# Two input-scale banks instead of four in the first FFN round, and the second convolution stage's output sums split between VectorE and GpSimd

## The chip, the cores and the metric

The kernel runs on one core of a Trainium2 chip. The metric is the device time of one execution in microseconds (us); for the kernel before it is the median of three runs. TensorE (PE) multiplies matrices into PSUM, VectorE (DVE) and ScalarE (ACT) work elementwise on PSUM and SBUF, GpSimd (POOL) elementwise on SBUF, and SyncE (SP) issues the DMAs. Engines wait for each other on counting semaphores that the kernel sets.

## The reference

A block of three residual parts over x of 2048 tokens by 1024 features, all in float32:

```
x = x + 0.5 * ffn(layernorm(x))
x = x + attention(layernorm(x))      # opens with a convolution over 3 tokens, 1024 -> 768
x = x + 0.5 * ffn(layernorm(x))      # the same weights as the first

def ffn(x):
    routing = softmax(x @ gate_w.T)                       # 8 experts
    in_scale, out_scale = routing @ in_channel_scale, routing @ out_channel_scale
    return x * in_scale @ sign(weight).T * out_scale + bias

def attention(x):
    q, k, v = split(conv3(x, conv_w) + conv_b, 3)         # 256 wide each
    # 16 heads of 64, causal softmax inside blocks of 128 tokens, then two projections
```

## The kernel before

Four phases run one after the other: FFN, convolution, attention, FFN. Tensors carry a prefix in the profile: `f_` for both FFNs, `c_` for the convolution, `a_` for attention. A float32 operand is split into a high part (rounded to the matmul's input format) and a low part (the rest), so that two or three fast matmuls give a product at nearly full precision.

**FFN.** Tokens go in 8 groups of 256. For each group TensorE transposes the normalised tokens (L587), ScalarE copies them to `f_xT` (L487), TensorE makes the router's logits (L597, L604), and the softmax's result comes back as `f_rT` (L499). Then, for each of 8 chunks k of 128 features, a chain of four steps makes the matmul's input: `in_scale` (L621, TensorE) writes the chunk's scales into 256 columns of a PSUM bank; `scale` (L343, VectorE) multiplies them by the tokens into the bank's other half; `high` (L504, ScalarE) rounds that half to `f_a_hi`; `low` (L348, VectorE) subtracts and leaves `f_a_lo`. VectorE's program has the order scale(k), low(k-1). The products follow (L638).

In every round but the first, `scale_bank` gives two banks, those of `f_p_s`, in turn, and in_scale(k) waits for low(k-2). This work for the next group lies between products of the group before. The first round has no products to lie between: it runs once at the start of each FFN, before the first product. There `scale_bank` gives four banks (the two of `f_p_s`, then `f_p_n` and `f_p_t`), and in_scale(k) waits for low(k-4) alone. Behind the chain ScalarE copies the next group's logits (L491), TensorE turns them (L604), makes an output scale (L626) and starts the products.

**Convolution.** The sequence is cut into groups of four outputs, which are computed from a few transformed products (stages j = 0, 1, 2), with 6 output chunks c in each stage: 18 units n. A unit makes two results in PSUM, `first` and `second`, in one of two pairs of banks, from 4 ring entries of filters (3 slots). An entry takes TensorE 12 matmuls. Filters of the second stage are the sum and difference of what GpSimd added (`outer_sum`, L785) and the middle tap: `sums(n)` (L989, L990, VectorE), then ScalarE rounds (`high`, L880) and VectorE subtracts (`finish`, L1000) into the ring. The filter half n arrives by DMA; its load waits until `sums(n-2)` is done in stage 2, and for `finish` in stage 3. In VectorE's program of stage 2 an odd n has finish(n,0), add((n-3)//2), finish(n,1).

`add(n)` takes a unit's results. In stage 2 ScalarE first writes two scaled copies of `second` to SBUF (`c_room`, L909, L910). VectorE then has six instructions: two that combine `first` with these copies and write back into the PSUM banks (L1024, L1025), and four that add the results to the four output planes `c_Y` (L1028 to L1032). TensorE may overwrite the banks after the sixth. GpSimd has only its `outer_sum` in this stage.

Between stage 2 and 3 VectorE and ScalarE also have 16 chunks of input data to split (L1012, L892), and SyncE loads four attention weights of 1 MB each (L837) behind the load of filter half 27, before that of half 28.

## Time and profile before

| | |
|---|---|
| median of 3 runs | 1117.16 us (1112.67 to 1117.47) |
| the profiled execution's own time, its span | 1117.16 us, 1115.4 us |
| mean granted TensorE clock | 0.931 of full speed |
| busy share of the span | PE 85%, DVE 64%, ACT 41%, POOL 33% |
| HBM read and written | 89.21 MB and 31.46 MB |

The span runs from the first to the last instruction; what lies around it is 1.76 us. The phases lie about at 0 to 250 us (FFN), 250 to 495 us (convolution), 495 to 910 us (attention) and from 910 us on (FFN). A matmul row's length is its own duration from first to last column; back-to-back matmuls overlap, so a row of 0.39 us can follow the one before by 0.23 us.

### The profile page before, as it was taken

How to read it: one execution, taken by the hardware profiler on the slowest of the kernel's cores; microseconds unless marked ns; L12 is line 12 of the kernel's file. 1: busy time of each engine (PE TensorE's matmuls, PEld its weight loads, DVE VectorE, ACT ScalarE, POOL GpSimd, SP SyncE). 2: the span in 40 equal slices, each digit the busy share in tenths (PEclk: the TensorE clock that was granted, in tenths of full speed). 3: DMA queues.
4: the chain of work that ended last, by engine and by line, in shares of the span. 5: the costliest groups of instructions: out<-in, count | busy, mean ns of one | idle time of the engine just before them, and what ended most of it. 6: DMA issues, size and time to landing. Idle time of an engine off the chain costs nothing. (4 is left out here: it accounts for less than half of the span.)

```text
span 1115.4 us, 15622 instructions
## 1 busy us (share of the span) xinstructions
PE 952.7 (85%) x4960; PEld 716.4 (64%) x4960; DVE 718.2 (64%) x1469; ACT 452.8 (41%) x1127; POOL 371.6 (33%) x305
## 2 busy tenths in 40 slices
PE   4898888868898998967978996998799746999997
PEld 3576666653335876845766785886678634678786
DVE  6677775477998885532774587288458447576652
ACT  3534444431244352323763454356345305433431
POOL 2245555564542200000223131133214411355555
PEclk9799999988999999986988997998899885999999
DMA  8333322322323426533002112121101258154243
GB/s 280 127 133 114 113 75 76 132 95 85 113 94 135 168 66 245 207 133 113 2 19 76 39 57 76 38 75 65 48 38 58 95 165 279 58 189 149 78 132 113
DMA packets 44781, 121.45 MB, mean 109 GB/s; under 512 B 5936, under 2 KB 18224, under 8 KB 43312
## 3 DMA queue, kind: packets, MB, share of 16 engines
q1 hardware_dynamic: 44720, 120.68, 31.4%
q8 instruction: 33, 0.54, 0.2%
q14 instruction: 28, 0.23, 0.1%
HBM read 89.21 MB, written 31.46 MB: 108 GB/s over the span
## 5 line engine op out<-in xcount | busy, mean ns | idle before, releaser
L638 PE MATMUL f_p_m<-f_wsign,f_a_hi 128*128 128x512 f32 x512 | 209.0, 408 | 0.0
L638 PE MATMUL f_p_m<-f_wsign,f_a_lo 128*128 128x512 f32 x512 | 203.1, 397 | 0.0
L1342 POOL TENSOR_TENSOR a_s<-a_s,a_sums 128x512 f32<-128x512 f32 x64 | 66.6, 1041 | 252.7 <-DVE a_sums L1481 252.7
L270 POOL TENSOR_TENSOR f_y<-f_y,f_res 128x512 f32<-128x512 f32 x64 | 82.7, 1293 | 147.3 <-DVE f_y L469 147.1
L1549 PE MATMUL a_p_g<-a_xs_hi,x_room 128*128 128x512 f32 x256 | 102.4, 448 | 22.8 <-DVE a_xs_lo L1433 22.2
L1397 ACT ACTIVATE a_s<-a_s,a_nmx 128x128 f32<-128x128 f32 x256 | 99.3, 390 | 39.1 <-DVE a_nmx L1477 39.0
L638 PEld LDWEIGHTS f_p_m<-f_wsign,f_a_hi 128*128 128x128 f32 x512 | 97.6, 191 | 22.6 <-issue 4.1
L638 PEld LDWEIGHTS f_p_m<-f_wsign,f_a_lo 128*128 128x128 f32 x512 | 97.7, 191 | 16.8
L1114 PE MATMUL c_p_m<-c_vf,c_ring_f 128*128 128x512 f32 x192 | 86.8, 609 | 9.5 <-DVE c_ring_f L792 6.4
L343 DVE TENSOR_TENSOR f_p_s<-f_xT,f_p_s 128x256 f32<-128x256 f32 x120 | 50.2, 424 | 65.9 <-PE f_p_s L621 65.2
L504 ACT CAST f_a_hi<-f_p_s 128x256 fp32r<-128x256 f32 x120 | 44.5, 376 | 107.1 <-DVE f_p_s L343 106.3
L1116 PE MATMUL c_p_m<-c_vh,c_ring 128*128 128x512 f32 x192 | 76.8, 400 | 8.7 <-DVE c_ring L1000 6.9
L267 POOL TENSOR_TENSOR f_res<-f_res,f_hbias 128x512 f32<-128x512 f32 x64 | 83.3, 1302 | 0.0
L1549 PEld LDWEIGHTS a_p_g<-a_xs_hi,x_room 128*128 128x128 f32 x256 | 53.0, 207 | 39.3 <-DVE a_xs_lo L1433 21.3
L469 DVE TENSOR_TENSOR f_y<-f_p_m,f_oscale 128x512 f32<-128x512 f32 x64 | 43.9, 686 | 51.3 <-PE f_p_m L638 51.3
L1117 PE MATMUL c_p_m<-c_vl,c_ring 128*128 128x512 f32 x192 | 76.0, 396 | 0.0
L1118 PE MATMUL c_p_m<-c_vh,c_ring 128*128 128x512 f32 x192 | 75.9, 396 | 0.0
L1114 PEld LDWEIGHTS c_p_m<-c_vf,c_ring_f 128*128 128x128 f32 x192 | 36.8, 195 | 59.1 <-issue 52.2
L487 ACT COPY f_xT<-f_p_t 128x512 f32<-128x512 f32 x56 | 33.1, 592 | 82.6 <-PE f_p_t L587 82.6
L587 PE MATMUL f_p_t<-ident,f_xin 128*128 128x128 f32 x224 | 38.6, 300 | 31.0 <-DVE f_xin L310 26.2
L785 POOL TENSOR_TENSOR c_raw<-c_raw 128x512 f32<-128x512 f32 x24 | 35.7, 1491 | 73.0 <-DMA c_raw<-in_conv_w_dram 48.8
L1472 DVE TENSOR_TENSOR a_s<-a_p_s,a_mask 128x512 f32<-128x512 f32 x64 | 43.7, 683 | 20.9 <-PE a_p_s L1573 20.8
(178 smaller groups left out, 2066.5 us busy)
## 6 DMA issues: line engine op xcount, KB each, us to landing
c_raw<-in_conv_w_dram SPq DMA_DIRECT2D x24, 768.0 KB, 4.3
f_y<-in_w_t_dram SPq DMA_DIRECT2D x16, 512.0 KB, 7.9
f_res<-in_x_dram SPq DMA_DIRECT2D x16, 512.0 KB, 3.8
x_after_ffn<-f_y SPq DMA_DIRECT2D x8, 1024.0 KB, 6.0
f_res<-x_after_attention SPq DMA_DIRECT2D x16, 512.0 KB, 3.9
out_dram<-f_y SPq DMA_DIRECT2D x8, 1024.0 KB, 6.1
f_xin<-in_x_dram SPq DMA_DIRECT2D x7, 1024.0 KB, 7.6
a_residual<-x_after_ffn SPq DMA_DIRECT2D x14, 512.0 KB, 3.5
```

What stands on the lines that cost most here:

```text
L267: pool.tensor_tensor(res[:, t, h], res[:, t, h], hbias[:, h], ALU.add).then_inc(res_biased, 1)
L270: pool.tensor_tensor(y[:, p, t, h], y[:, p, t, h], res[:, t, h], ALU.add).then_inc(y_done, 1)
L343: dve.tensor_tensor(bank[:, FTOK:HALF], xT[:, p, k, :], bank[:, 0:FTOK], ALU.mult).then_inc(scaled, 1)
L504: act.copy(a_hi[:, p, k, :], scale_bank(g, k)[:, FTOK:HALF]).then_inc(hi_done, 1)
L638: last = pe.matmul(p_m[:, q % 2, :], part[:, p, k, q // 2 * P:q // 2 * P + P], wsign[:, k, q % 2 * HALF:q % 2 * HALF + HALF], start=(k == ...
L1114: last = pe.matmul(out, ring_f[:, slot, 0, cols], vf[:, f, k, :], start=start, stop=stop)
L1116: pe.matmul(out, ring[:, slot, 0, cols], vh[:, f, k, :], start=start, stop=False)
L1117: pe.matmul(out, ring[:, slot, 0, cols], vl[:, f, k, :], start=False, stop=False)
L1118: last = pe.matmul(out, ring[:, slot, 1, cols], vh[:, f, k, :], start=False, stop=stop)
L1342: pool.tensor_tensor(s[:, r], s[:, r], sums[:, r].unsqueeze(2).broadcast_to([P, 4, P]), ALU.mult).then_inc(probs_ready, 1)
L1397: done = act.activation(s[:, r, h, :], s[:, r, h, :], ACT.Exp, bias=nmx[:, r, h:h + 1], scale=SCALE, accum_out=sums[:, r, h:h + 1])
L1549: mm = pe.matmul(p_g[:, bank, :], a, b, start=n == 0, stop=n == len(pairs) - 1)
```

## The change

Three parts. (1) `scale_bank` is gone: the first round uses the two banks of `f_p_s` as all others do, and in_scale(k) waits for low(k-2) there too. The waits that kept `f_p_n` and `f_p_t` apart from their other users go with it. (2) In stage 2 of the convolution the combined results go to `c_room` in SBUF instead of PSUM; VectorE adds two of the four planes and GpSimd the other two, between its `outer_sum`s. (3) TensorE may overwrite `first` after the two combining instructions, and `second` after ScalarE's copies. SyncE's stores wait for the split counters.

```diff
-        def scale_bank(g, k):
-            if first_round(g):
-                return (p_s[:, 0, :], p_s[:, 1, :], p_n[:], p_t[:])[k % 4]
-            return p_s[:, k % 2, :]
...
                 def in_scale(g, p, k):
                     pe.wait_ge(r_copied, g + 1)
-                    if not first_round(g):
-                        wait(pe, lo_done, 8 * g + k - 1)
-                    elif k >= 2:
-                        wait(pe, lo_done, k - 3)
-                        pe.wait_ge(t_copied, 8)
-                    pe.matmul(scale_bank(g, k)[:, 0:FTOK], ics3[:, k * P:k * P + P], rT[:, p, :],
+                    wait(pe, lo_done, 8 * g + k - 1)
+                    pe.matmul(p_s[:, k % 2, 0:FTOK], ics3[:, k * P:k * P + P], rT[:, p, :],
...
+                def add(c):                                   # GpSimd
+                    n = NCH + c
+                    pool.wait_ge(first_taken, n + 1)
+                    pool.wait_ge(y_scaled, c + 1)
+                    pool.tensor_tensor(Y[:, c, 2], room[:, 0], Y[:, c, 2], ALU.add)
+                    pool.tensor_tensor(Y[:, c, 3], room[:, 1], Y[:, c, 3], ALU.add).then_inc(out_added, 1)
...
                 for n in range(2 * NCH, 4 * NCH):
                     conv.outer_sum(pool, n)
+                    if n % 2 == 0 and n >= 2 * NCH + 4:
+                        add((n - 2 * NCH - 4) // 2)
+                add(NCH - 2)
+                add(NCH - 1)
...
                     if j == 1:                                # ScalarE, before it writes room
-                        wait(act, y_added, 5 * c - 3)
+                        wait(act, y_added, 2 * c)
+                        wait(act, out_added, c)
...
                     if j == 1:                                # VectorE
                         dve.wait_ge(second_taken, n + 1)
-                        dve.scalar_tensor_tensor(second, first, -1.0 / 6, room[:, 1], ALU.mult, ALU.subtract).then_inc(y_added, 1)
-                        dve.scalar_tensor_tensor(first, first, -1.0 / 6, room[:, 0], ALU.mult, ALU.add).then_inc(y_added, 1)
+                        dve.scalar_tensor_tensor(room[:, 0], first, -1.0 / 6, room[:, 0], ALU.mult, ALU.add)
+                        dve.scalar_tensor_tensor(room[:, 1], first, -1.0 / 6, room[:, 1], ALU.mult, ALU.subtract).then_inc(first_taken, 1)
+                        dve.wait_ge(first_taken, n + 1)
                         dve.wait_ge(y_scaled, c + 1)
-                        dve.wait_ge(y_added, 5 * c + 1)
-                        dve.tensor_tensor(Y[:, c, 1], second, Y[:, c, 1], ALU.add).then_inc(y_added, 1)
-                        dve.tensor_tensor(Y[:, c, 3], second, Y[:, c, 3], ALU.add).then_inc(y_added, 1)
-                        dve.wait_ge(y_added, 5 * c + 2)
-                        dve.tensor_tensor(Y[:, c, 0], first, Y[:, c, 0], ALU.add).then_inc(y_added, 1)
-                        dve.tensor_tensor(Y[:, c, 2], first, Y[:, c, 2], ALU.add).then_inc(first_taken, 1)
+                        dve.tensor_tensor(Y[:, c, 0], room[:, 0], Y[:, c, 0], ALU.add).then_inc(y_added, 1)
+                        dve.tensor_tensor(Y[:, c, 1], room[:, 1], Y[:, c, 1], ALU.add).then_inc(y_added, 1)
...
                     if f == 0:                                # TensorE, before it overwrites a bank
                         pe.wait_ge(first_taken, n - 1)
-                    elif n - 2 < NCH:
+                    elif n - 2 < 2 * NCH:
                         pe.wait_ge(second_taken, n - 1)
-                    elif n - 2 < 2 * NCH:
-                        pe.wait_ge(first_taken, n - 1)
```

TensorE's program in the first round of an FFN, before the change (lines of the kernel before; the first two rows are in_scale for k = 0 and 1, the last the first product):

```order
L621 MATMUL f_p_s<-f_rT,f_ics 128x256 [waits f1_r_copied]
L597 MATMUL f_p_r<-f_xT,f_gateT 32x256 [waits f1_r_copied,f1_t_copied]
L597 MATMUL f_p_r<-f_xT,f_gateT 32x256 x7
L621 MATMUL f_p_n<-f_rT,f_ics 128x256 [waits f1_t_copied,f1_r_copied]
L621 MATMUL f_p_t<-f_rT,f_ics 128x256 [waits f1_t_copied,f1_r_copied]
L621 MATMUL f_p_s<-f_rT,f_ics 128x256 [waits f1_t_copied,f1_lo_done,f1_r_copied] x2
L621 MATMUL f_p_n<-f_rT,f_ics 128x256 [waits f1_t_copied,f1_lo_done,f1_r_copied]
L621 MATMUL f_p_t<-f_rT,f_ics 128x256 [waits f1_t_copied,f1_lo_done,f1_r_copied]
L604 MATMUL f_p_r<-f_four_to_one,f_logT 128x8 [waits f1_l_copied]
```

And now, in the changed kernel's own line numbers (L608 is in_scale, L588 the logits, L595 their turn):

```order
L608 MATMUL f_p_s<-f_rT,f_ics 128x256 [waits f1_r_copied]
L588 MATMUL f_p_r<-f_xT,f_gateT 32x256 [waits f1_r_copied,f1_t_copied]
L588 MATMUL f_p_r<-f_xT,f_gateT 32x256 x7
L608 MATMUL f_p_s<-f_rT,f_ics 128x256 [waits f1_lo_done,f1_r_copied] x6
L595 MATMUL f_p_r<-f_four_to_one,f_logT 128x8 [waits f1_l_copied]
```

The order is the same; six in_scales wait for a `low` where four did, and each for one two chunks back.

GpSimd's program in stage 2, now (L772 is `outer_sum`, L853 and L854 the new additions; before, `outer_sum` stood alone in all these rows); the first row is outer_sum(16):

```order
L772 TENSOR_TENSOR c_raw<-c_raw 128x512 [waits c_raw_loaded0]
L853 TENSOR_TENSOR c_Y<-c_room,c_Y 128x512 [waits c_y_scaled,c_first_taken]
L854 TENSOR_TENSOR c_Y<-c_room,c_Y 128x512
L772 TENSOR_TENSOR c_raw<-c_raw 128x512 [waits c_raw_loaded1]
L772 TENSOR_TENSOR c_raw<-c_raw 128x512 [waits c_raw_loaded0]
L853 TENSOR_TENSOR c_Y<-c_room,c_Y 128x512 [waits c_y_scaled,c_first_taken]
L854 TENSOR_TENSOR c_Y<-c_room,c_Y 128x512
```

outer_sum(17) and outer_sum(18) now stand behind an addition that waits for VectorE.

VectorE's program there, now, from a unit's combining instructions to the next unit's (L1025, L1026 combine; L1029, L1030 add planes; L1001 is `finish`, L990 and L991 are `sums`):

```order
L1025 SCALAR_TENSOR_TENSOR c_room<-c_p_m,c_room 128x512 [waits c_second_taken]
L1026 SCALAR_TENSOR_TENSOR c_room<-c_p_m,c_room 128x512
L1029 TENSOR_TENSOR c_Y<-c_room,c_Y 128x512 [waits c_y_scaled,c_first_taken]
L1030 TENSOR_TENSOR c_Y<-c_room,c_Y 128x512
L1001 TENSOR_TENSOR c_ring<-c_p_u,c_ring 128x512 [waits c_filter_high]
L990 TENSOR_TENSOR c_p_u<-c_raw 128x512 [waits c_filter_ready,c_outer_made]
L991 TENSOR_TENSOR c_p_u<-c_raw 128x512
L1001 TENSOR_TENSOR c_ring<-c_p_u,c_ring 128x512 [waits c_filter_high] x2
L990 TENSOR_TENSOR c_p_u<-c_raw 128x512 [waits c_filter_ready,c_outer_made]
L991 TENSOR_TENSOR c_p_u<-c_raw 128x512
L1001 TENSOR_TENSOR c_ring<-c_p_u,c_ring 128x512 [waits c_filter_high]
```

Two plane additions are left where four stood, and both now read two SBUF tensors, where each read one from PSUM (`c_p_m`).

## Rows read from the trace of the kernel before

**Rows 1.** The page, part 1: busy time, share of the span and instructions of each engine.

```profile
PE 952.7 (85%) x4960; PEld 716.4 (64%) x4960; DVE 718.2 (64%) x1469; ACT 452.8 (41%) x1127; POOL 371.6 (33%) x305
```

**Rows 2.** Timeline, first FFN: start us, us, engine, line, operation [idle before <-releaser].

```profile
29.02 0.58 PE L621 MATMUL f_p_n<-f_rT,f_ics 128*128 128x256 f32 x1
29.08 0.42 DVE L348 TENSOR_TENSOR f_a_lo<-f_p_s,f_a_hi 128x256 fp32r<-128x256 f32 x1
29.64 0.43 DVE L343 TENSOR_TENSOR f_p_n<-f_xT,f_p_n 128x256 f32<-128x256 f32 x1
...
32.96 0.42 DVE L343 TENSOR_TENSOR f_p_t<-f_xT,f_p_t 128x256 f32<-128x256 f32 x1
...
34.12 1.02 PE L604 MATMUL f_p_r<-f_four_to_one,f_logT 128*128 128x8 f32 x4 [1.74 <-ACT f_logT L491]
...
38.98 0.90 PE L587 MATMUL f_p_t<-ident,f_xin 128*128 128x128 f32 x4
```

**Rows 3.** Timeline, a later round of the same FFN, where two banks are used.

```profile
73.72 0.41 DVE L348 TENSOR_TENSOR f_a_lo<-f_p_s,f_a_hi 128x256 fp32r<-128x256 f32 x1
...
74.61 0.43 DVE L343 TENSOR_TENSOR f_p_s<-f_xT,f_p_s 128x256 f32<-128x256 f32 x1 [0.48 <-PE f_p_s L621]
```

**Rows 4.** Timeline, first round of the second FFN.

```profile
939.67 0.42 DVE L348 TENSOR_TENSOR f_a_lo<-f_p_s,f_a_hi 128x256 fp32r<-128x256 f32 x1
...
943.80 0.42 DVE L343 TENSOR_TENSOR f_p_t<-f_xT,f_p_t 128x256 f32<-128x256 f32 x1
```

**Rows 5.** Windows: stretch, busy PE, PEld, DVE, ACT, POOL, granted clock, DMA share, GB/s.

```profile
32.00:34.00 2.00, 0.37 (x1) 0.08 (x1) 1.88 (x7) 1.33 (x5) 0.00 (x0) 0.50 0.99 393
942.00:944.00 2.00, 0.71 (x2) 0.34 (x2) 2.00 (x7) 1.12 (x3) 0.00 (x0) 1.00 0.99 379
944.00:946.00 2.00, 1.05 (x5) 1.05 (x6) 1.89 (x5) 1.75 (x4) 0.00 (x0) 0.53 0.48 195
```

**Rows 6.** Timeline, first convolution stage and its end: DVE and POOL.

```profile
276.08 1.26 POOL L785 TENSOR_TENSOR c_raw<-c_raw 128x512 f32<-128x512 f32 x1 [0.55 <-ACT c_raw L777]
276.13 1.76 DVE L792 SCALAR_TENSOR_TENSOR c_ring_f<-c_raw 128x512 f32<-128x512 f32 x1
...
341.24 1.54 POOL L785 TENSOR_TENSOR c_raw<-c_raw 128x512 f32<-128x512 f32 x1 [2.72 <-DMA c_raw<-in_conv_w_dram]
341.56 1.75 DVE L1007 TENSOR_TENSOR c_vl<-X,c_vh 128x512 fp32r<-128x512 f32 x1
```

**Rows 7.** Timeline, second convolution stage: DVE, POOL and ACT.

```profile
365.10 0.70 DVE L1024 SCALAR_TENSOR_TENSOR c_p_m<-c_p_m,c_room 128x512 f32<-128x512 f32 x1 [0.48 <-ACT c_room L910]
...
368.54 1.29 POOL L785 TENSOR_TENSOR c_raw<-c_raw 128x512 f32<-128x512 f32 x1 [1.75 <-DMA c_raw<-in_conv_w_dram]
368.70 0.68 DVE L1000 TENSOR_TENSOR c_ring<-c_p_u,c_ring 128x512 fp32r<-128x512 f32 x1
374.19 0.59 ACT L880 CAST c_ring<-c_p_u 128x512 fp32r<-128x512 f32 x1 [2.13 <-DVE c_p_u L990]
375.98 0.70 DVE L1024 SCALAR_TENSOR_TENSOR c_p_m<-c_p_m,c_room 128x512 f32<-128x512 f32 x1 [0.48 <-ACT c_room L910]
```

**Rows 8.** Timeline, from the second convolution stage into the third.

```profile
418.41 0.47 PE L1116 MATMUL c_p_m<-c_vh,c_ring 128*128 128x512 f32 x1 [0.79 <-issue]
...
424.25 0.69 DVE L1024 SCALAR_TENSOR_TENSOR c_p_m<-c_p_m,c_room 128x512 f32<-128x512 f32 x1
427.85 1.28 DVE L1000 TENSOR_TENSOR c_ring<-c_raw,c_ring 128x512 fp32r<-128x512 f32 x2
428.58 0.50 PE L1116 MATMUL c_p_m<-c_vh,c_ring 128*128 128x512 f32 x1 [1.17 <-DVE c_ring L1000]
430.97 0.43 SPq L772 DMA_DIRECT2D c_raw<-in_conv_w_dram  x1
444.31 1.14 ACT L880 CAST c_ring<-c_raw 128x512 fp32r<-128x512 f32 x2 [9.27 <-DMA c_raw<-in_conv_w_dram]
445.80 0.76 PE L1116 MATMUL c_p_m<-c_vh,c_ring 128*128 128x512 f32 x1 [3.31 <-DVE c_ring L1000]
```

More of the change, by code:

```diff
@@ L339, in scale @@
                 def scale(g, p, k):
-                    bank = scale_bank(g, k)
                     dve.wait_ge(s_full, 8 * g + k + 1)
-                    dve.tensor_tensor(bank[:, FTOK:HALF], xT[:, p, k, :], bank[:, 0:FTOK], ALU.mult).then_inc(scaled, 1)
+                    dve.tensor_tensor(p_s[:, k % 2, FTOK:HALF], xT[:, p, k, :], p_s[:, k % 2, 0:FTOK], ALU.mult).then_inc(scaled, 1)
                 def low(g, p, k):
@@ L347, in low @@
                     wait(dve, m_full, 4 * g - 4)
-                    dve.tensor_tensor(a_lo[:, p, k, :], scale_bank(g, k)[:, FTOK:HALF], a_hi[:, p, k, :].bitcast(F32),
+                    dve.tensor_tensor(a_lo[:, p, k, :], p_s[:, k % 2, FTOK:HALF], a_hi[:, p, k, :].bitcast(F32),
                                       ALU.subtract).then_inc(lo_done, 1)
@@ L503, in high @@
                     wait(act, m_full, 4 * g - 4)
-                    act.copy(a_hi[:, p, k, :], scale_bank(g, k)[:, FTOK:HALF]).then_inc(hi_done, 1)
+                    act.copy(a_hi[:, p, k, :], p_s[:, k % 2, FTOK:HALF]).then_inc(hi_done, 1)
                 def sign_w(k):
@@ L580, in transposes @@
                     wait(pe, t_copied, 4 * g + q - two)
-                    if isinstance(g, int) and g == 2 and q == 0:
-                        pe.wait_ge(lo_done, 8)
                     bank = p_n if two and q % 2 else p_t
@@ L804, in conv_phase @@
     first_taken, second_taken = sem("first_taken"), sem("second_taken")
-    y_scaled, y_added, y_final = sem("y_scaled"), sem("y_added"), sem("y_final")
+    y_scaled, y_added, out_added, y_final = sem("y_scaled"), sem("y_added"), sem("out_added"), sem("y_final")
     y_stored = sem("y_stored")
@@ L841, in _ @@
                         sp.wait_ge(first_taken, 2 * NCH + c + 1)
-                        sp.wait_ge(y_added, 5 * c + 5)
+                        sp.wait_ge(y_added, 2 * c + 2)
+                        sp.wait_ge(out_added, c + 1)
                         sp.dma_start(Yd[c], Y[:, c].rearrange("p s m -> p (s m)")).then_inc(y_stored, 16)
@@ L846, in _ @@
                     sp.wait_ge(first_taken, 2 * NCH + c + 1)
-                    sp.wait_ge(y_added, 5 * c + 5)
+                    sp.wait_ge(y_added, 2 * c + 2)
+                    sp.wait_ge(out_added, c + 1)
                     sp.dma_start(Yd[c], Y[:, c].rearrange("p s m -> p (s m)")).then_inc(y_stored, 16)
@@ L1023, in add @@
                         dve.wait_ge(second_taken, n + 1)
-                        dve.scalar_tensor_tensor(second, first, -1.0 / 6, room[:, 1], ALU.mult, ALU.subtract).then_inc(y_added, 1)
-                        dve.scalar_tensor_tensor(first, first, -1.0 / 6, room[:, 0], ALU.mult, ALU.add).then_inc(y_added, 1)
+                        dve.scalar_tensor_tensor(room[:, 0], first, -1.0 / 6, room[:, 0], ALU.mult, ALU.add)
+                        dve.scalar_tensor_tensor(room[:, 1], first, -1.0 / 6, room[:, 1], ALU.mult, ALU.subtract).then_inc(first_taken, 1)
+                        dve.wait_ge(first_taken, n + 1)
                         dve.wait_ge(y_scaled, c + 1)
-                        dve.wait_ge(y_added, 5 * c + 1)
-                        dve.tensor_tensor(Y[:, c, 1], second, Y[:, c, 1], ALU.add).then_inc(y_added, 1)
-                        dve.tensor_tensor(Y[:, c, 3], second, Y[:, c, 3], ALU.add).then_inc(y_added, 1)
-                        dve.wait_ge(y_added, 5 * c + 2)
-                        dve.tensor_tensor(Y[:, c, 0], first, Y[:, c, 0], ALU.add).then_inc(y_added, 1)
-                        dve.tensor_tensor(Y[:, c, 2], first, Y[:, c, 2], ALU.add).then_inc(first_taken, 1)
+                        dve.tensor_tensor(Y[:, c, 0], room[:, 0], Y[:, c, 0], ALU.add).then_inc(y_added, 1)
+                        dve.tensor_tensor(Y[:, c, 1], room[:, 1], Y[:, c, 1], ALU.add).then_inc(y_added, 1)
                     if j == 2:
                         dve.wait_ge(chunk_used, 16 * n + 16)
-                        dve.wait_ge(y_added, 5 * c + 5)
+                        dve.wait_ge(y_added, 2 * c + 1)
+                        dve.wait_ge(out_added, c + 1)
                         dve.scalar_tensor_tensor(Y[:, c, 0], first, 0.25, Y[:, c, 0], ALU.mult, ALU.add).then_inc(first_taken, 1)
```

## The prediction, made before the changed kernel ran

> **What bounds the kernel now.** The page's first part comes first: TensorE is busy for 85% of the span [rows 1], and where it isn't, each gap has one cause. So an edit counts where it lengthens or shortens a gap of TensorE. The change touches two places in each of which TensorE hardly works: the first round of each FFN, where the timeline shows no product yet, and the second convolution stage with its end. I read the timeline of both, engine by engine.
>
> In the first round of the first FFN the reader is to see that VectorE sets the pace. TensorE issued in_scale(2) at 29.02, before low(0) ended at 29.08 + 0.42 = 29.50, into a third bank; scale(2) began at 29.64, scale(7) at 32.96 [rows 2]. That is 5 steps in 3.32 us, 0.66 each, and one `scale` and one `low` are queued at 0.33 each. The granted clock was 0.50, 1.2 GHz [rows 5]. Behind scale(7) come high(7), ScalarE's copy of the logits, then TensorE's L604, which sat idle 1.74 us for that copy [rows 2], and all first products. Nothing of the kernel runs ahead of this chain, so what it loses the program loses.
>
> In stage 2 of the convolution TensorE runs without a gap: two units' combining instructions began at 365.10 and 375.98, 10.88 us apart [rows 7], which is 48 matmuls at 0.227. VectorE has slack there. At the end of the stage it has none: TensorE sat idle 0.79 at 418.41 and 1.17 at 428.58 for a ring entry that VectorE finished late, and 3.31 at 445.80 for filter half 28, which was issued at 430.97 behind the attention weights and reached ScalarE only at 444.31 [rows 8].
>
> **Part 1, two banks in the first round.** Now in_scale(k) waits for low(k-2), and VectorE's program has low(k-2) right before scale(k). So VectorE waits for the whole way over TensorE and back. This is seen in a later round, where two banks are in use: low ended at 73.72 + 0.41 = 74.13 and the next scale began at 74.61, 0.48 later, at 2.4 GHz [rows 3]. At 1.2 GHz the matmul is longer: from 29.02 to the scale at 29.64 it is 0.62 [rows 2], and with 0.05 to 0.1 for the semaphore 0.69. A step is then 0.33 (scale) + 0.42 (low) + 0.69 = 1.44 us at 1.2 GHz and 1.23 at 2.4 GHz, against 0.66.
> - First FFN: scale(2) at 29.50 + 0.69 = 30.19, scale(7) five steps later at 37.39, against 32.96 [rows 2]: +4.4 us. The clock was low in this stretch [rows 5] and TensorE gets even less to do.
> - Second FFN: low(0) ended at 940.09 [rows 4]. scale(2) at 940.8; steps 3 to 5 at 1.23, since the clock was 1.00 in 942 to 944, and 6 and 7 at 1.44, since it was 0.53 in 944 to 946 [rows 5]: scale(7) at 947.3 against 943.80 [rows 4], +3.5 us.
> Together +7.9 us. Bounds: five steps that cost only 0.57 more and a free start are 2.9 per FFN, five at 0.78 and a full start 4.4; so +5.8 to +8.8. The dropped waits on `f_p_n` and `f_p_t` were long fulfilled and give nothing. Nothing covers this: ScalarE's signs of the weights, the normalising and the second softmax stand behind the chain on their own engines and move with it.
>
> **Part 2, the plane additions.** On paper VectorE loses two instructions of 0.6 in each unit, less about 0.1 for waiting for its own combining instruction: 1.1 us. In stage 2 this meets slack. At its end it would count twice, for add(10) and add(11), since VectorE works there without a pause: half 28 would be issued 2.1 us sooner and TensorE's start at 445.80 come 2.1 us sooner. That is the gain side, -2.1.
>
> But the additions left on VectorE now read two SBUF tensors, and GpSimd starts its own in the same moment, on the same semaphore. What such a meeting costs is in the trace. GpSimd began at 276.08 and ended at 277.34; a VectorE instruction with two SBUF operands that began at 276.13 took 1.76 instead of 0.68 and ended at 277.89, 0.55 after GpSimd. Where VectorE was first, GpSimd's instruction took 1.54 instead of 1.29, and VectorE's next, 1.75 [rows 6]. Beside a VectorE instruction with one operand in PSUM nothing is lost: 0.68 at 368.70 within GpSimd's 368.54 to 369.83 [rows 7]. So in a meeting of two-SBUF instructions one waits for the other. (The Trainium skill says the same in "SBUF — State Buffer", section "SBUF: two separate sides": the port pair that VectorE and GpSimd share is an exclusive lock for the whole instruction, which a VectorE op with two SBUF inputs needs too; by that rule the offload is no gain, without it the sum is -2.1. The trace agrees with the rule at 276.13, 1.76 us.)
>
> Counted from T, the start of a unit's first combining instruction, with 1.15 us for a GpSimd instruction after VectorE lets go and 0.55 for VectorE after GpSimd:
> - combining 0 to 1.30; VectorE's first addition to 2.05; GpSimd's first to 3.15; VectorE's second to 3.7; GpSimd's second to 4.8;
> - finish (one operand in PSUM) runs meanwhile, but sums(17) needs outer_sum(17), which now stands behind GpSimd's additions: to 6.05. outer_sum(18) follows without a pause, to 7.35, as its filter has landed; it meets sums(17), whose first half then ends at 7.9, the second at 8.5;
> - two finishes to 9.7, sums(18) to 10.9, one finish to 11.5: the next T.
> VectorE and GpSimd together need 11.55 us for what TensorE does in 10.88. The first needed entry would be ready at 365.10 + 9.15 = 374.25, and TensorE wanted it at about 374.19, when it let go of the entry before [rows 7]. From there the lateness grows by 0.67 per unit over two more units (after the fourth, no second outer_sum stands in the way): 0.1, 0.8, 1.5. TensorE ends stage 2 1.5 us late.
>
> At the end of the stage: after add(10) the first data split, an instruction with two SBUF operands, meets GpSimd's second addition, and ends at T + 5.3 to 5.5 instead of T + 4.8: +0.6. After add(11) the same meets the finish that TensorE waited for at 428.58; its source is now SBUF, so it ends at T + 5.3, where it ended 427.85 + 0.68 - 424.25 = 4.28 after T [rows 8]: +1.0. Half 28 and all behind it come later by 1.5 + 0.6 + 1.0 = 3.1 us, and from 445.80 on TensorE has only its own work. Bounds for the convolution: -2.1 (no meeting costs) to +6, if a cycle takes one more 1.07 of blocking (three cycles, 3.2, less what doesn't reach TensorE). I take +3.1, nearest to rows 6.
>
> **Part 3, banks released sooner** is worth nothing: six instructions from 365.10 are over by 368.8, and TensorE returns to those banks at about 374.19, when the unit between is done [rows 7]; at the stage's end it waits for ring entries, not for banks.
>
> **Sum.** +7.9 + 3.1 = +11.0 us on a profiled span of 1115.4: 1126.4, and with the 1.76 around it 1128.2. The profiled execution is the median of the runs (1117.16), so no correction is due.
>
> **The rivals.**
> - *No port to share.* The additions on VectorE and GpSimd run side by side. The convolution gains 2.1; 1117.2 + 7.9 - 2.1 = 1123.0. For it: GpSimd is idle for most of this stage. Against it: both rows at 1.75 us.
> - *Not slower: the clock pays the chain back.* From 34.12 to 38.98 the first FFN's TensorE worked at 1.2 GHz on the logits and the first products [rows 2], 4.9 us; at 2.4 GHz that is 2.4 shorter, and the second FFN has the same block. If the evenly spread matmuls of the longer chain bring the clock up where a burst and a pause did not, the steps cost 1.23 (+3.2 in the first FFN, +3.1 in the second) and the block behind them runs fast (-2.4 each): +1.5 for both FFNs, +4.6 with the convolution, 1121.8, within 0.5%. It decides if the granted clock reads above 0.8 over the chain and the eight products behind it. Against it: in 32 to 34 it read 0.50 [rows 5], and TensorE will have less to do per us than in the burst before that.
> - *The cycle is tighter than I count.* Each unit of stage 2 costs 12.2 instead of 11.55, with another addition blocked: convolution +5.5, in all 1130.6.
>
> **How the numbers follow.** The least that a measurement of this kernel tells from no change is about 0.5%, 5.6 us. The forecast has 0.64, the tighter cycle 0.12, no shared port 0.15, the clock 0.09. Forecast and tighter cycle are slower by more than 0.5%; no shared port, at +5.8, stands on the edge and is halved, with 0.01 more on the fast side from errors in both FFN terms: slower 0.85, same 0.13, faster 0.02. Range: from the clock and no-port cases to the tighter cycle with the FFN bound of +8.8, 1121 to 1133; it leaves out about 1 in 10 on each side.
>
> **What would show it.** In each first round, scale(2) to scale(7) 6.2 to 7.2 us instead of 3.3, with VectorE idle 0.5 to 0.7 before each scale, waiting for TensorE. In stage 2, VectorE's additions at 1.2 to 1.8 us instead of 0.68, GpSimd's above 1.29, T to T about 11.5, and TensorE idle before some entries. The third stage's start at 445.80 late by the first FFN's 4.4 plus 3.1. I am wrong if additions stay at 0.68 while GpSimd works, or if a first round's five steps take under 5 us.

## The result, and the profile after

The changed kernel took 1122.77 us (median of 6 runs, 1120.59 to 1127.39), the kernel before 1117.32 in the same comparison (6 runs, 1112.67 to 1118.70): ratio 1.0065, 95% interval 1.0036 to 1.0095. It is slower: the whole interval lies above 1. Whether by more than the 0.5% of the prediction stays open, since the interval holds 1.005 and the two medians alone give 1.0049. The forecast was 1128.2 with a range of 1121 to 1133. The profiled execution has a span of 1121.8 and its own time is 1123.61. All ratios compare fast runs with fast runs, which leaves out one run of the kernel before, of 2338.01 us, beside g1 and g2.

The busy rows of the page, to be held against [rows 1] (engine, busy us, share, instructions):

```profile
PE 948.7 (85%) x4960; PEld 712.6 (64%) x4960; DVE 726.2 (65%) x1457; ACT 452.8 (40%) x1127; POOL 394.2 (35%) x317
```

**The chain of the first FFN** in the timeline of the kernel after (start, us, engine, line, operation, out<-in, idle before and what ended it). It answers [rows 2]:

```profile
29.86 0.42 DVE L341 TENSOR_TENSOR f_a_lo<-f_p_s,f_a_hi 128x256 fp32r<-128x256 f32 x1
30.43 0.55 PE L608 MATMUL f_p_s<-f_rT,f_ics 128*128 128x256 f32 x1 [0.41 <-DVE f_a_lo L341]
31.02 0.43 DVE L336 TENSOR_TENSOR f_p_s<-f_xT,f_p_s 128x256 f32<-128x256 f32 x1 [0.73 <-PE f_p_s L608]
31.36 0.41 DVE L341 TENSOR_TENSOR f_a_lo<-f_p_s,f_a_hi 128x256 fp32r<-128x256 f32 x1
31.91 0.55 PE L608 MATMUL f_p_s<-f_rT,f_ics 128*128 128x256 f32 x1 [0.94 <-DVE f_a_lo L341]
32.50 0.43 DVE L336 TENSOR_TENSOR f_p_s<-f_xT,f_p_s 128x256 f32<-128x256 f32 x1 [0.73 <-PE f_p_s L608]
...
38.46 0.43 DVE L336 TENSOR_TENSOR f_p_s<-f_xT,f_p_s 128x256 f32<-128x256 f32 x1 [0.74 <-PE f_p_s L608]
...
39.62 0.59 PE L595 MATMUL f_p_r<-f_four_to_one,f_logT 128*128 128x8 f32 x2 [1.20 <-ACT f_logT L484]
```

The two engines now take turns: low ends at 29.86 + 0.42 = 30.28, the matmul runs from 30.43 to 30.98, scale starts at 31.02. VectorE is idle 0.73 before each scale and TensorE 0.94 before each matmul but the first. scale(2) to scale(7) is 7.44 us, five steps of 1.488, where it was 3.32. In the second FFN the same two instructions stand at 942.65 and 950.09, again 7.44 us, and the granted clock (the third figure from a row's end) was 0.50, 1.2 GHz, throughout, where [rows 5] had 1.00 in 942 to 944:

```profile
32.00:34.00 2.00, 1.02 (x2) 0.46 (x2) 0.76 (x3) 0.37 (x1) 0.00 (x0) 0.50 1.03 414
942.00:944.00 2.00, 1.01 (x2) 0.57 (x2) 0.75 (x2) 0.37 (x1) 0.00 (x0) 0.50 1.02 404
944.00:946.00 2.00, 0.65 (x2) 0.29 (x1) 1.13 (x4) 0.37 (x1) 0.00 (x0) 0.50 0.97 387
```

**Stage 2 of the convolution**, one unit from its first combining instruction T = 369.31; it answers [rows 6, 7]:

```profile
369.31 0.69 DVE L1025 SCALAR_TENSOR_TENSOR c_room<-c_p_m,c_room 128x512 f32<-128x512 f32 x1 [0.43 <-ACT c_room L911]
...
370.63 0.69 DVE L1029 TENSOR_TENSOR c_Y<-c_room,c_Y 128x512 f32<-128x512 f32 x1
370.68 1.80 POOL L853 TENSOR_TENSOR c_Y<-c_room,c_Y 128x512 f32<-128x512 f32 x1 [3.73 <-DVE c_room L1026]
371.24 1.78 DVE L1030 TENSOR_TENSOR c_Y<-c_room,c_Y 128x512 f32<-128x512 f32 x1
372.44 1.74 POOL L854 TENSOR_TENSOR c_Y<-c_room,c_Y 128x512 f32<-128x512 f32 x1
372.95 0.68 DVE L1001 TENSOR_TENSOR c_ring<-c_p_u,c_ring 128x512 fp32r<-128x512 f32 x1
374.14 2.54 POOL L772 TENSOR_TENSOR c_raw<-c_raw 128x512 f32<-128x512 f32 x2
375.46 1.77 DVE L990 TENSOR_TENSOR c_p_u<-c_raw 128x512 f32<-128x512 f32 x1 [1.83 <-POOL c_raw L772]
```

All but VectorE's first addition are stretched: each waits for the other engine's, and the four end one after another at T + 2.01, 3.17, 3.71 and 4.87. GpSimd's outer_sum for the next sums comes behind them. The next unit's T is 380.94, 11.63 us later, where two units were 10.88 apart.

**The end of stage 2**, which answers [rows 8]:

```profile
432.36 1.80 POOL L853 TENSOR_TENSOR c_Y<-c_room,c_Y 128x512 f32<-128x512 f32 x1 [12.66 <-DVE c_room L1026]
432.93 1.79 DVE L1030 TENSOR_TENSOR c_Y<-c_room,c_Y 128x512 f32<-128x512 f32 x1
434.13 1.71 POOL L854 TENSOR_TENSOR c_Y<-c_room,c_Y 128x512 f32<-128x512 f32 x1
434.64 1.75 DVE L1001 TENSOR_TENSOR c_ring<-c_raw,c_ring 128x512 fp32r<-128x512 f32 x1
```

And TensorE's three waits there, which were 0.79, 1.17 and 3.31:

```profile
425.17 0.47 PE L1113 MATMUL c_p_m<-c_vh,c_ring 128*128 128x512 f32 x1 [1.34 <-issue]
436.44 0.50 PE L1113 MATMUL c_p_m<-c_vh,c_ring 128*128 128x512 f32 x1 [2.24 <-DVE c_ring L1001]
454.14 0.77 PE L1113 MATMUL c_p_m<-c_vh,c_ring 128*128 128x512 f32 x1 [3.81 <-DVE c_ring L1001]
```

The finish at 434.64 took 1.75 us: it met GpSimd's second addition, which ended at 434.13 + 1.71 = 435.84. The finish ended at 436.39, and TensorE started at 436.44.

**Where the 6.4 us of the two spans went**, from the starts of the same instructions in both traces (after minus before): to the first FFN's first scale +0.8; its chain to the logits' turn +4.7 (5.90 to 10.62); to the start of stage 2 -1.3; stage 2 to TensorE's restart at filter half 28 +4.1 (98.30 to 102.42); to the last plane addition +1.1 (46.0 to 47.1); attention, from there to the last group's store, **-5.8** (406.8 to 401.1); to the second FFN's first scale -1.9; its chain +4.5 (6.14 to 10.64); the rest +0.1. The edited places lost 13.3 us. About half of that came back in places where no instruction was changed, most of it in attention. These are two single profiles; a second pair follows below.

### The profile page after: what moved, and what is told of

It is laid out like the page before. It is cut to its first block and busy times, and to the rows that moved or that the text cites. A ratio compares the mean times of both kernels' runs of the same rounds, so it can differ in the third digit from the quotient of the medians.

```text
span 1121.8 us, 15634 instructions
## 1 busy us (share of the span) xinstructions
PE 948.7 (85%) x4960; PEld 712.6 (64%) x4960; DVE 726.2 (65%) x1457; ACT 452.8 (40%) x1127; POOL 394.2 (35%) x317
## 5 line engine op out<-in xcount | busy, mean ns | idle before, releaser
L336 DVE TENSOR_TENSOR f_p_s<-f_xT,f_p_s 128x256 f32<-128x256 f32 x128 | 53.7, 425 | 74.2 <-PE f_p_s L608 73.5
L497 ACT CAST f_a_hi<-f_p_s 128x256 fp32r<-128x256 f32 x128 | 47.5, 375 | 119.6 <-DVE f_p_s L336 118.8
L608 PE MATMUL f_p_s<-f_rT,f_ics 128*128 128x256 f32 x128 | 41.3, 326 | 24.1 <-DVE f_a_lo L341 21.4
L578 PEld LDWEIGHTS f_p_t<-ident,f_xin 128*128 128x128 f32 x224 | 29.3, 153 | 43.2 <-DVE f_xin L304 29.4
```

The costliest lines, as they stand in the source:

```text
L336: dve.tensor_tensor(p_s[:, k % 2, FTOK:HALF], xT[:, p, k, :], p_s[:, k % 2, 0:FTOK], ALU.mult).then_inc(scaled, 1)
L578: last = pe.transpose(bank[:, c * FTOK + t * P:c * FTOK + t * P + P], xin[:, p, t, k * P:k * P + P], ident[:])
```

## The experiments

All ratios are to the kernel before, on the same chip: e1 to e4 ran on one chip, f1 to f4, g1 and g2 on a second, h1 and h2 on a third. "Stage 2 to restart" is from its first matmul to TensorE's start at filter half 28.

**1. The FFN's part alone, the convolution's part alone, and each kernel again.** e1 has the new FFN and the old convolution, e2 the reverse.

```diff
  e1: -  return (p_s[:, 0, :], p_s[:, 1, :], p_n[:], p_t[:])[k % 4]     (first round)
      +  return p_s[:, k % 2, :]        and in_scale(k) waits for low(k-2)
  e2: +  the split add(n), GpSimd's add(c) and their semaphores; FFN as before
```

> Only part 1: two banks in the first round of both FFNs, the convolution as before. Theory (each chain step waits for the way over TensorE and back): in each FFN scale(2) to scale(7) takes 7.2 to 7.4 us at 1.2 GHz against 3.3, the logits' turn behind it comes 4.4 to 4.8 us later in the first FFN and 3.5 to 5 in the second; whole kernel +6 to +9 us. Rival (the clock pays it back): the stretch from the logits' turn to the first transposes behind the eight first products shrinks from 4.9 us to under 3, whole kernel +2 to +4 us.

> Only parts 2 and 3: the convolution as changed, the FFNs with four banks. Theory (VectorE and GpSimd block each other on instructions with two SBUF operands): units of stage 2 begin 11.6 us apart, from the first matmul of stage 2 to the restart at filter half 28 it takes 3 to 4.5 us longer than the 98.3 us of before, whole kernel +3 to +4.5 us. Rival (no cost of meeting): 10.9 us apart, the stretch 2.1 us shorter, whole kernel -2 us.

> The kernel before, unchanged, for a second profile. In the first pair of profiles the attention phase, in which both kernels run the same instructions, took 4.7 us less in the changed kernel (from the convolution's last plane addition to the second FFN's first transpose: 427.6 before, 422.8 after). Theory (the granted clock falls and rises at other places from execution to execution): this stretch differs here from 427.6 by 1 us or more, with another mean granted clock. Rival (it belongs to the kernel): 427.6 within 0.5 us.

> The changed kernel again, for a second profile. Theory (clock from execution to execution): the attention stretch is off 422.8 by 1 us or more, while the convolution's stretch (first matmul of stage 2 to the restart at filter half 28) and the two chains repeat within 0.5 us. Rival (it belongs to the kernel): 422.8 within 0.5 us.

e1: 1125.59 us, ratio 1.0115 [1.0066, 1.0165], but of 4 runs only. Both chains 10.64 us, stage 2 to restart 98.59. From the logits' turn at 40.43 to the first transposes at 45.29 it took 4.86 us, as in the kernel before (34.12 to 38.98), where the rival asked for under 3. e2: 1114.80, ratio 1.0008 [0.9984, 1.0032]. Both chains 6.14, units 11.62 apart, stage 2 to restart 102.13. TensorE's waits at the stage's end, first of e1, then of e2:

```profile
425.38 0.47 PE L1103 MATMUL c_p_m<-c_vh,c_ring 128*128 128x512 f32 x1 [0.79 <-issue]
435.55 0.50 PE L1103 MATMUL c_p_m<-c_vh,c_ring 128*128 128x512 f32 x1 [1.16 <-DVE c_ring L987]
```

```profile
424.21 0.47 PE L1126 MATMUL c_p_m<-c_vh,c_ring 128*128 128x512 f32 x1 [1.34 <-issue]
435.49 0.50 PE L1126 MATMUL c_p_m<-c_vh,c_ring 128*128 128x512 f32 x1 [2.24 <-DVE c_ring L1014]
```

Each part's loss stays in its own place, at the size it has in the whole change. But e2 as a whole lost 0.9 us with 3.8 us lost in the convolution: its attention took 401.4 us, and e1's 403.3. The kernel before took 404.7 in its second profile (e3, one run of 1114.89), the kernel after 401.6 (e4, 1122.31). Against their first profiles that is 2.1 less and 0.5 more: the kernel before moved as the theory said, the kernel after stayed as the rival said. In this second pair the edited places lost 12.7 us (4.5 in each chain, 98.31 against 101.99 from stage 2 to restart), the spans differ by 7.4, and attention gave back 3.1, not 5.8. So there is a give-back again, but nearly half of attention's part in the first pair was that one profile of the kernel before.

**2. Three banks in the first round** (f1).

```diff
-                return (p_s[:, 0, :], p_s[:, 1, :], p_n[:], p_t[:])[k % 4]
+                return (p_s[:, 0, :], p_s[:, 1, :], p_n[:])[k % 3]
-                        wait(pe, lo_done, k - 3)
+                        wait(pe, lo_done, k - 2)
```

> The kernel before with three banks in the first round (the two of p_s, then p_n; in_scale(k) waits for low(k-3)). From the first scale to the logits' turn it takes 6.1 us with four banks and 10.6 with two. Theory (a chain step is the way from low over TensorE to scale, 0.73 us, and with a third bank VectorE has one more pair of instructions to do meanwhile): two steps together take 0.42 + 0.73 + 0.33 = 1.48 us, 0.74 each, so 6.4 to 6.7 us, and the whole kernel +0.5 to +1 us, too little to measure. Rival (each bank taken away costs alike): half way, 8.4 us, whole kernel +4 to +5 us.

1114.18 us, ratio 1.0001 [0.9978, 1.0024]; chain 6.39. The timeline of the first round, two steps:

```profile
31.83 0.42 DVE L348 TENSOR_TENSOR f_a_lo<-f_p_s,f_a_hi 128x256 fp32r<-128x256 f32 x1
32.16 0.42 DVE L343 TENSOR_TENSOR f_p_s<-f_xT,f_p_s 128x256 f32<-128x256 f32 x1
...
33.00 0.55 PE L621 MATMUL f_p_n<-f_rT,f_ics 128*128 128x256 f32 x1
...
33.61 0.42 DVE L343 TENSOR_TENSOR f_p_n<-f_xT,f_p_n 128x256 f32<-128x256 f32 x1
```

With one bank more than two the matmul runs beside VectorE's next scale and low, and VectorE shows almost no idle time in these two steps. So it is the direct round trip that costs, not the number of banks as such. The five steps from scale(2) to scale(7) take 3.57 us with three banks, 3.32 with four and 7.44 with two. The chain as a whole took 5.67 to 6.15 us in the ten profiles with four banks, so its 6.39 here is known to be worse by 0.2 to 0.7 us, against 4.7 with two banks.

**3. The meetings of VectorE and GpSimd** (f2, f3; both have the FFN of before and the new convolution). f2 leaves out GpSimd's two additions to planes 2 and 3 altogether. f3 has them one outer_sum later:

```diff
  f2: -  pool.tensor_tensor(Y[:, c, 2], room[:, 0], Y[:, c, 2], ALU.add)
      -  pool.tensor_tensor(Y[:, c, 3], room[:, 1], Y[:, c, 3], ALU.add)
  f3: -  if n % 2 == 0 and n >= 2 * NCH + 4:   add((n - 2 * NCH - 4) // 2)
      +  if n % 2 and n >= 2 * NCH + 5:        add((n - 2 * NCH - 5) // 2)
```

> FFNs as before; the convolution as changed, but GpSimd's two plane additions are left out (planes 2 and 3 of the second stage's result are then not added, so the output differs). Theory (the loss is the meeting of GpSimd and VectorE): VectorE's additions take 0.68 us, stage 2 runs at 10.9 us per unit, and from stage 2's first matmul to the restart at filter half 28 it takes 96.2 us, 2.1 less than before's 98.3 and 5.9 less than 102.1 with the additions. Rival (it is VectorE's reading from SBUF and its wait for its own combining instructions): additions of 0.8 us or more without GpSimd, 98 us or more.

> FFNs as before; the convolution as changed, but GpSimd's additions for unit c stand behind outer_sum(17 + 2c) instead of outer_sum(16 + 2c). Theory (what stretches stage 2 is that sums(17) waits for an outer_sum behind the additions): units 10.9 us apart again though VectorE's second addition still takes 1.8 us; the 2.0 us of drift in stage 2 are gone, the 2.1 at the stage's end stay: 100.4 us from stage 2's first matmul to the restart. Rival (the blocked additions by themselves make VectorE too slow): 11.3 us or more apart, 101.5 to 102 us.

f2: 1109.71 us, 0.9968 [0.9947, 0.9988]; units 10.88 apart, stage 2 to restart 96.51, 1.8 below before: VectorE's saved instructions are worth nearly what the prediction's gain side said (2.1), as long as nobody meets them. VectorE's two additions in f2:

```profile
369.14 0.73 DVE L1028 TENSOR_TENSOR c_Y<-c_room,c_Y 128x512 f32<-128x512 f32 x1
369.79 0.68 DVE L1029 TENSOR_TENSOR c_Y<-c_room,c_Y 128x512 f32<-128x512 f32 x1
```

f3: 1114.49, 1.0012 [0.9991, 1.0032]; units 10.88, 11.33, 11.21 and 10.69 apart, stage 2 to restart 100.39. The total is the theory's; two of the four distances are the rival's 11.3. With outer_sum first, most of the drift is gone (0.6 of 2.0 us is left), but the first two waits at the end are those of the change, and the additions still meet:

```profile
375.85 1.29 POOL L785 TENSOR_TENSOR c_raw<-c_raw 128x512 f32<-128x512 f32 x1 [4.95 <-DMA c_raw<-in_conv_w_dram]
375.88 1.80 DVE L1042 TENSOR_TENSOR c_Y<-c_room,c_Y 128x512 f32<-128x512 f32 x1
377.09 1.74 POOL L866 TENSOR_TENSOR c_Y<-c_room,c_Y 128x512 f32<-128x512 f32 x1
377.61 1.77 DVE L1043 TENSOR_TENSOR c_Y<-c_room,c_Y 128x512 f32<-128x512 f32 x1
...
418.13 0.47 PE L1126 MATMUL c_p_m<-c_vh,c_ring 128*128 128x512 f32 x1 [1.34 <-issue]
429.40 0.50 PE L1126 MATMUL c_p_m<-c_vh,c_ring 128*128 128x512 f32 x1 [2.28 <-DVE c_ring L1014]
```

From f2 (96.51) to f3 (100.39) to e2 (102.13): the meetings cost 5.6 us, of which the order of outer_sum is 1.7.

**4. Another order at the stage's end** (f4). The kernel before, with VectorE's finishes there each behind four data splits, and add(11) behind the finish that TensorE waits for:

```diff
-                for r in range(8):
+                for r in range(4):
                     third_low(r)
+                finish(4 * NCH, 0)
+                for r in range(4, 8):
+                    third_low(r)
+                finish(4 * NCH, 1)
+                ...                      # r 8 to 11, finish(25, 0), r 12 to 15
+                finish(4 * NCH + 1, 1)
+                add(2 * NCH - 1)
```

> The kernel before, but at the end of stage 2 VectorE's program is written in another order: the four finishes of filter halves 24 and 25 come each as soon as the third stage's data split of their quarter is done (after 4, 8, 12 and 16 of the 16 instructions), and add(11) follows them instead of standing before the last. Theory (TensorE waits at 418.41 and 428.58 for entries that VectorE finishes late, and the attention weights and filter half 28 are issued only behind the last of them): both gaps go (2.5 us), the weights are issued 3 us sooner, and from stage 2's first matmul to the restart at filter half 28 it takes 93.5 to 95.5 us instead of 98.3; whole kernel -3 to -4.5 us. Rival (the restart is bound by the transfer of the weights, which only begins sooner by what the last finish gains, or add(11), now later, holds up the banks): the gap before the restart grows by what the others lose, 97.5 to 98.3 us, no change.

1107.74 us, ratio 0.9952 [0.9933, 0.9971], faster than the kernel before; stage 2 to restart 94.87, 3.4 less than before. Of the two waits that the theory wanted gone, one is (0.79) and one is left at 0.77 instead of 1.17; the third is 1.98 instead of 3.31. TensorE's waits:

```profile
429.37 0.47 PE L1121 MATMUL c_p_m<-c_vh,c_ring 128*128 128x512 f32 x1 [0.77 <-DVE c_ring L1000]
442.47 0.77 PE L1121 MATMUL c_p_m<-c_vh,c_ring 128*128 128x512 f32 x1 [1.98 <-DVE c_ring L1000]
```

The reading that the stage's end is where VectorE sets the pace is confirmed from the other side: the same instructions, no offload, only their order.

**5. The kernel before, only later.** Scratch additions of 128x256 in VectorE's program at the start of stage 2 (10, 5, 18 and 22 of them), with one memset that clears the scratch tile, delay everything behind and change nothing else.

```diff
+                for i in range(10):
+                    dve.wait_ge(idled, i + 1)
+                    dve.tensor_tensor(conv.idle[:], conv.idle[:], conv.idle[:], ALU.add).then_inc(idled, 1)
                 sums(2 * NCH)
```

> The kernel before, with ten additions on a scratch tile of 128x256 put into VectorE's program at the start of the second convolution stage, where TensorE waits for VectorE; a row of this size took 0.43 us, with a semaphore between them about 0.5 each, so stage 2 and all behind it start 4 to 5 us later. Nothing is changed behind that. The theory is that the kernel changed lost less than its local losses because the granted clock in the attention phase depends on when that phase starts: then an attention phase that starts 4 to 5 us later (at 510 to 511) takes 401 to 402.5 us from the convolution's last addition to the last group's store, and the kernel as a whole loses 1 to 2.5 us (about 1.001 to 1.002). The rival is that the start doesn't matter and the gain came with the changed kernel's convolution: then the attention phase takes 403 to 407 and the whole loses the 4 to 5 us (1.004).

> The same with five such additions, 2 to 2.5 us. If the start alone decides, the attention phase shortens by a part of that or not at all, and the whole loses 1 to 2.5 us; the rival says 2 to 2.5 us. It shows with the run of ten whether the phase's time moves with its start at all: by the rival both have 403 to 407 without order.

> The kernel before with eighteen of the scratch additions at the start of the second convolution stage. With ten they took 0.45 us each and delayed the combining in stage 2 by about 3.2, since some of the blocked work behind them was then quicker; so eighteen delay it by 6.5 to 7. The attention phase then starts at 510 to 511 in a kernel whose convolution and instructions are otherwise those of before. If the late start is what gave the kernel changed its attention phase of 401 us, it takes 401 to 402.5 here, and the whole loses 3 to 4.5. The rival: 403 to 407, and the whole loses the 6.5 to 7 (1.006).

> The same with twenty-two, a delay of 8.5 to 9 us, so that attention starts at 512 to 513, where it does in the kernel changed. By the late start: the low stretches of the granted clock after the start as in the kernel changed (no dip about 8 us after the start, 6.8 us for the next), attention 401 to 402, the whole loses 4 to 6 us. The rival: attention 403 to 407, the whole loses 8.5 to 9 (1.008).

The delay is read between two rows that stand close on either side of the scratch additions: VectorE's last filter write of stage 1 (L792 before, L793 in these runs) and the second-stage unit's T. In before it is this row and 365.10 of [rows 7], 28.84 us apart:

```profile
336.26 0.69 DVE L792 SCALAR_TENSOR_TENSOR c_ring_f<-c_raw 128x512 f32<-128x512 f32 x1 [0.47 <-PE c_p_m L1114]
```

In the ten profiles without scratch additions the distance is 28.4 to 29.1. In g1 and then in g2:

```profile
335.47 0.69 DVE L793 SCALAR_TENSOR_TENSOR c_ring_f<-c_raw 128x512 f32<-128x512 f32 x1 [0.43 <-PE c_p_m L1120]
336.08 6.48 DVE L1054 TENSOR_TENSOR c_idle<-c_idle 128x256 f32<-128x256 f32 x10
...
367.12 0.70 DVE L1026 SCALAR_TENSOR_TENSOR c_p_m<-c_p_m,c_room 128x512 f32<-128x512 f32 x1 [0.33 <-ACT c_room L912]
```

```profile
337.34 0.69 DVE L793 SCALAR_TENSOR_TENSOR c_ring_f<-c_raw 128x512 f32<-128x512 f32 x1 [0.47 <-PE c_p_m L1120]
337.95 3.21 DVE L1054 TENSOR_TENSOR c_idle<-c_idle 128x256 f32<-128x256 f32 x5
...
367.38 0.70 DVE L1026 SCALAR_TENSOR_TENSOR c_p_m<-c_p_m,c_room 128x512 f32<-128x512 f32 x1 [0.35 <-ACT c_room L912]
```

Attention is read from the last plane addition to the last group's first store.

| run | the two rows, us | delay, us | attention's first matmul at | attention, us | whole, ratio | in us |
|---|---|---|---|---|---|---|
| g1 (10) | 335.47, 367.12 | 2.81 | 505.7 | 406.6 | 1.0014 [0.9988, 1.0040] | +1.6 (-1.3 to 4.5) |
| g2 (5) | 337.34, 367.38 | 1.20 | 505.8 | 404.2 | 0.9982 [0.9960, 1.0004] | -2.0 (-4.5 to 0.4) |
| h1 (18) | 336.06, 371.38 | 6.48 | 511.3 | 403.2 | 1.0048 [1.0029, 1.0067] | +5.3 (3.2 to 7.5) |
| h2 (22) | 339.02, 376.21 | 8.35 | 514.5 | 400.0 | 1.0069 [1.0045, 1.0092] | +7.7 (5.0 to 10.2) |

g1 and g2 missed their aim: they delayed by 2.8 and 1.2 us instead of 4 to 5 and 2 to 2.5, and neither reached a start at 510. The ten additions took 6.48 us, but VectorE had waited 1.60 us for GpSimd at this place before, and the eight data splits behind took 4.90 us instead of 7.04, since the two outer_sums that they had met now met the scratch additions. g1 and g2 say only that at one start, 505.7, attention takes 404.2 or 406.6. h1 lies between the two theories, its attention at the rival's edge. h2 has the late start with the convolution of before, and the shortest attention of all, so the new convolution is not needed for a short one. Its low stretch of the clock after the first was 10.2 us, though, not the 6.8 that I expected. In the ratios no payback shows: three of the four delays lie inside the interval of their whole, and only g2's 1.20 lies above its own (up to 0.4).

## Why the prediction was right, and where it was too high

**The FFN chains: right in mechanism, 1.3 us too low.** VectorE waits for TensorE and back. A step is 1.488, against 1.44: from the end of low to the scale it is 0.74 (30.28 to 31.02), not 0.69, since TensorE itself starts 0.15 after low's end. First FFN +4.7, against +4.4. The 7.44 us from scale(2) to scale(7) are more than the 6.2 to 7.2 that I had named as the sign. In the second FFN, +4.5 against +3.5: I took the clock of the old chain for three steps, but the new chain ran wholly at 1.2 GHz (0.50 in both windows), with TensorE idle 0.94 of 1.49 us. The 1.00 of [rows 5] in 942 to 944 was not even a lasting trait of the old chain: in e2, which has it at the same place, the same window read 0.50. The rival by which the clock would pay the chain back is refuted in its own place: it asked for above 0.8 over the chain, and the row says 0.50; and in e1 the block behind the chain took 4.86 us, not 2.4 less.

**The convolution: right in mechanism, 1.0 us too low.** The four additions of a unit end at T + 2.01, 3.17, 3.71, 4.87, where I had 2.05, 3.15, 3.7, 4.8; T to T was 11.63 against 11.55. From stage 2's start to T of add(10) the trace has 61.1 before and 63.1 after: three units of 11.63, 11.61 and 11.62 instead of 10.88, then one of 10.65. That is a drift of 2.0 where I had 1.5; I had let the first unit's lateness vanish in slack that wasn't there. The end: +0.6 at add(10) as forecast, +1.1 at add(11) against +1.0, and 0.5 more on the way to half 28, for a third wait that I had held constant (3.31 became 3.81). TensorE's start at 445.80 came at 454.14, 8.3 us late, where I had 4.4 + 3.1 = 7.5. No shared port is refuted at 370.63 to 374.18 and by f2; the tighter cycle, 12.2 us, by 11.63. (The rule of the Trainium skill's "SBUF — State Buffer", "SBUF: two separate sides", that this port pair is a lock for a whole instruction, agrees with the 1.78 and 1.80 us. It says nothing on who comes next when both have work queued, and that sets the order here: the engines took turns, instruction by instruction.) That taking turns is no rule of its own. In this row of the kernel before, an outer_sum beside seven VectorE instructions that followed each other without a wait (257.83 to 262.12) ended only after the last of them:

```profile
257.89 5.37 POOL L785 TENSOR_TENSOR c_raw<-c_raw 128x512 f32<-128x512 f32 x1 [10.60 <-ACT c_raw L777]
```

**The step that failed: "what it loses the program loses".** The edited places lost 13.3 us, more than the 11.0 forecast, and the kernel only 6.4 in the profiles, 7.3 (4.0 to 10.6) by the ratio. I added the losses as if everything behind them ran as before. It didn't. The rows that show it are each kernel's windows of 100 us from about attention's first matmul (TensorE's granted clock is again the third figure from the end). Of before, which starts at 503.5:

```profile
503.00:603.00 100.00, 81.41 (x498) 63.64 (x499) 57.17 (x108) 53.89 (x166) 16.66 (x16) 0.83 0.19 56
603.00:703.00 100.00, 91.04 (x576) 73.14 (x576) 64.34 (x115) 49.04 (x164) 30.69 (x22) 0.93 0.18 61
```

Of after, which starts at 512.7:

```profile
512.00:612.00 100.00, 81.24 (x517) 63.75 (x518) 61.14 (x110) 55.84 (x169) 19.66 (x18) 0.89 0.19 59
612.00:712.00 100.00, 90.83 (x581) 72.99 (x580) 62.56 (x113) 49.41 (x163) 29.99 (x21) 0.95 0.17 59
```

The same program gets a granted clock of 0.83 in its first 100 us in one place and 0.89 in another, and does 517 matmuls instead of 498 with the same busy time. An estimate from these two figures: 0.06 of 100 us is 6 us of TensorE's time at full clock, and attention was 5.8 us shorter. In the next 100 us the two read 0.93 and 0.95. Attention opens with much idle time of TensorE, and the clock there goes up and down several times. In before it rose at 517.4, fell at 520.9 and rose again at 524.3; in after it rose at 521.3 and stayed up until 579.4.

The same window of all fourteen profiles, from the whole microsecond before attention's first matmul:

| run | first matmul at | granted clock, first 100 us | attention, us |
|---|---|---|---|
| after | 512.7 | 0.89 | 401.1 |
| e2 | 511.7 | 0.88 | 401.4 |
| e4 | 512.8 | 0.88 | 401.6 |
| h2 | 514.5 | 0.87 | 400.0 |
| f2 | 505.3 | 0.87 | 403.2 |
| f4 | 499.9 | 0.86 | 402.0 |
| h1 | 511.3 | 0.86 | 403.2 |
| e1 | 510.4 | 0.86 | 403.3 |
| g2 | 505.8 | 0.85 | 404.2 |
| f3 | 505.5 | 0.85 | 404.2 |
| e3 | 505.7 | 0.85 | 404.7 |
| f1 | 507.0 | 0.85 | 405.4 |
| before | 503.5 | 0.83 | 406.8 |
| g1 | 505.7 | 0.82 | 406.6 |

Attention's length goes with this clock: 400.0 to 403.3 us where it read 0.86 or more, 404.2 to 406.8 where it read 0.85 or less. It goes less clearly with the start. The six that start at 510.4 or later took 400.0 to 403.3, the eight at 507.0 or before 402.0 to 406.8. The late ones tend to be short, but the earliest of all, f4, is short as well. Its last plane addition and its last group's first store:

```profile
488.49 0.68 DVE L1037 TENSOR_TENSOR c_Y<-c_p_m,c_Y 128x512 f32<-128x512 f32 x1
...
890.53 3.06 SPq L1282 DMA_DIRECT2D x_after_attention<-a_residual  x2
```

So a late start is not needed. Nor are start and chip apart: f and g, on one chip, all start early, h1 and h2, on another, late; only among e1 to e4, on one chip, do both stand (404.7 against 401.4 to 403.3). So the profiles show that attention's time and the clock go together. What sets this clock they don't show: the start, the state that the clock is in when the kernel starts, or something else that varies from run to run. Much does vary: over the fourteen profiles the first FFN's first scale stood at 27.0 to 30.2 us, the way from attention's last group to the second FFN's first scale took 37.2 to 41.8 us (so the -1.9 there means little), and the runs of the kernel before went from 1109.31 to 1120.78 beside f1 to f4.

Over all runs the shortfall is clear of the noise in the whole change alone: 13.3 us lost locally (12.7 in the second pair) against 7.3 (4.0 to 10.6). In e2 and g2 it is so by a hair: 3.8 against 0.9 (-1.8 to 3.6), and 1.2 against -2.0 (-4.5 to 0.4). The other delays cost what they were, within their intervals. e1's 9.5 show as 12.8 (7.3 to 18.4), f4's gain of 3.4 as 5.3 (3.2 to 7.4), f2's of 1.8 as 3.6 (1.3 to 5.9). How much of a local change reaches the end is therefore known here to some 3 us, and for the whole change 6 us are missing; the cause within the clock stays open.

The range held partly by luck. Two errors had opposite signs: the edited places lost 2.3 us more than forecast, and some 6 us of it did not reach the end. The measured 1122.77 lies nearest to the number of a rival, no shared port with 1123.0, whose mechanism the rows refute. The range's lower end took in a payback by the clock, but put it at the wrong place: in the FFN, where it was refuted, and not in attention, which starts some 75 us behind the last edited instruction.

## What to carry to other kernels

With two banks between two engines, look at which instruction stands between the release of a bank and its next use: if it is none, both engines wait for the whole round trip, and one more bank removes nearly all of it (6.39 us against 10.6). Before work with two SBUF operands is moved from VectorE to GpSimd, look whether VectorE itself has such work at that moment. Here it had, and four additions that ended 3.7 us after T on VectorE alone (368.10 + 0.68 - 365.10) ended at 4.9, and what GpSimd had to do next was late. Where TensorE's clock goes up and down, add local losses to know where they are, but hold 3 us and more of a 1100 us kernel for what the clock does behind them, and repeat the profile before explaining the difference. Measure a delay between two rows close to it: the distance from the first FFN's transposes to T, some 326 us long, went from 324.9 to 327.8 in the ten profiles without scratch additions, and by it g2's five additions would seem to delay more (3.7) than g1's ten (3.2).

## What the runs showed that I had not expected

- The same attention instructions took 400.0 to 406.8 us over fourteen profiles; the clock of the first 100 us read 0.82 and 0.83 in the two longest, 0.86 to 0.89 in the eight shortest.
- Ten scratch additions took 6.48 us and delayed the convolution by 2.8: they filled a wait of 1.60 and took two meetings with GpSimd on themselves. What a delay costs depends on whom it makes one miss.
- Another order of some twenty VectorE instructions at one stage's end gained 3.4 us locally (f4), more than the offload gains where it meets nobody (1.8, f2).
